# Grouped attention: queries for four batches at once, and values times probabilities in three rounded products

## The reference, cut to what matters

```python
def _L2_xattn_ref(text_hidden, vision_tokens, vision_mask, Wq, Wk, Wv, Wo):
    ...
    q = (text_hidden @ Wq).reshape(B, T_text, N_HEADS, HEAD_DIM).transpose(0, 2, 1, 3)
    k = (vision_tokens @ Wk).reshape(B, T_vis, N_KV_HEADS, HEAD_DIM).transpose(0, 2, 1, 3)
    v = (vision_tokens @ Wv).reshape(B, T_vis, N_KV_HEADS, HEAD_DIM).transpose(0, 2, 1, 3)
    ...
    scores = jnp.einsum('bhtd,bhsd->bhts', q, k) / scale
    mask = vision_mask[:, None, None, :]
    scores = jnp.where(mask, scores, -jnp.inf)
    attn = jax.nn.softmax(scores, axis=-1)
    ...
    out = jnp.einsum('bhts,bhsd->bhtd', attn, v)
    out = out.transpose(0, 2, 1, 3).reshape(B, T_text, N_HEADS * HEAD_DIM)
    return out @ Wo
```

## Time and profile before

| | us |
|---|---|
| median of 3 runs | 1918.61 |
| lowest, highest | 1918.14, 1919.21 |
| the profiled execution's own time | 1918.69 |
| its span | 1916.8 |
| first block of grouped attention | 1239.9 to 1258.2 |
| second block, first query matmul | 1258.24 |
| second block, first scores | 1269.92 |
| layer norm after it begins | 1449.9 |

### The profile page before, as it was taken

The page is one execution under the profiler, slowest core; times in us unless marked ns, Lnnn a source line. Parts: engine busy times, 40 slices in busy tenths (PEclk is TensorE's granted clock), DMA queues, the critical chain, the costliest instruction groups (busy, mean ns, idle before and its releaser), DMA issues. The chain is left out here.

```text
span 1916.8 us, 32156 instructions
## 1 busy us (share of the span) xinstructions
PE 1604.5 (84%) x11677; PEld 1182.8 (62%) x11677; DVE 1411.8 (74%) x2370; ACT 802.5 (42%) x1261; POOL 528.5 (28%) x594
## 2 busy tenths in 40 slices
PE   7899999999898986465858779899995998898864
PEld 5678888888784663122536445687773885645631
DVE  3299999999565855899487764556684995657697
ACT  3367666766232545333234312433342002425544
POOL 2234443433242511577112103200000330414200
PEclk9899999999898988688979989999997999998985
DMA  3000000000000000000100020000001220010000
GB/s 149 28 29 27 25 25 27 20 26 14 12 1 13 2 8 36 0 0 0 47 3 2 28 110 4 12 18 12 12 19 55 73 70 28 4 59 2 1 1 23
DMA packets 18145, 49.24 MB, mean 26 GB/s; under 512 B 2035, under 2 KB 8436, under 8 KB 16886
## 3 DMA queue, kind: packets, MB, share of 16 engines
q1 hardware_dynamic: 18038, 47.78, 7.3%
HBM read 46.73 MB, written 1.05 MB: 25 GB/s over the span
## 5 line engine op out<-in xcount | busy, mean ns | idle before, releaser
L2183 DVE SCALAR_TENSOR_TENSOR arena<-psum,arena 128x1016 f32<-128x1016 f32 (+2 forms) x240 | 303.4, 1265 | 35.9 <-ACT arena L2120 30.2
L902 DVE TENSOR_REDUCE limits<-psum 128x4 f32<-128x512 f32 (+2 forms) x256 | 147.9, 619 | 81.7 <-PE psum L757 49.2
L2029 PE MATMUL psum<-ssm_XT_hi,ssm_split 128*128 128x512 f32 x640 | 194.6, 407 | 11.7 <-POOL ssm_split L1988 5.7
L870 ACT ACTIVATE PT<-psum 128x1024 f32<-128x1024 f32 x112 | 108.6, 1021 | 115.0 <-PE psum L788 115.0
L2029 PEld LDWEIGHTS psum<-ssm_XT_hi,ssm_split 128*128 128x128 f32 x640 | 116.3, 192 | 37.0 <-POOL ssm_split L1988 10.9
L2120 ACT ACTIVATE arena<-psum,arena 128x1024 f32<-128x1024 f32 x80 | 89.1, 1114 | 106.0 <-PE psum L2029 104.7
L2606 PE MATMUL psum<-expert,x 128*128 128x256 f16 x1024 | 114.0, 276 | 16.7 <-POOL expert L2592 16.7
L757 PE MATMUL psum<-K,QR 32*128 32x256 f32 (+1 forms) x320 | 118.4, 443 | 7.8 <-DVE limits L902 6.4
L2783 POOL TENSOR_TENSOR fed<-dtx,b_all 128x1024 f32<-128x1024 f32 x32 | 103.2, 3243 | 65.1 <-DVE state L2852 33.4
L2606 PEld LDWEIGHTS psum<-expert,x 128*128 128x128 f16 x1024 | 101.1, 99 | 29.5 <-issue 16.8
L2619 DVE SCALAR_TENSOR_TENSOR acc<-psum,gate_now,acc 128x256 f32<-128x256 f32 x256 | 111.9, 483 | 7.7 <-PE psum L2606 7.6
(11 more groups left out here) (446 smaller groups left out, 3857.8 us busy)
## 6 DMA issues: line engine op xcount, KB each, us to landing
expert_mask<-in_expert_masks SPq DMA_DIRECT2D x32, 256.0 KB, 2.6
arena<-in_ssm_in SPq DMA_DIRECT2D x16, 384.0 KB, 3.0
arena<-in_L_xattn SPq DMA_DIRECT2D x1, 5120.0 KB, 15.8
arena<-in_ssm_in SPq DMA_DIRECT2D x16, 256.0 KB, 3.0
arena<-in_L_ffn SPq DMA_DIRECT2D x1, 2592.0 KB, 8.9
arena<-in_L_xattn SPq DMA_DIRECT2D x2, 1280.0 KB, 9.6
arena<-in_L_ffn SPq DMA_DIRECT2D x1, 2176.0 KB, 8.4
ssm_gated<-in_ssm_z SPq DMA_DIRECT2D x4, 512.0 KB, 5.8
```

Of the source, the lines that this page charges most:

```text
L870: nc.scalar.activation(PT[:, u % 2, 2 * k:2 * k + 2, :, :].rearrange("p r h q -> p (r h q)"), p.psum[:, (2 + 2 * k) * 512:(4 + 2 * k) * 51 ...
L902: ins = nc.vector.tensor_reduce(limits[:, u % 2, r, :, k], score_bank(r)[:, :].rearrange("p (h k) -> p h k", h=4)[:, :, lo:hi], AX.X, ALU. ...
L2029: ins = nc.tensor.matmul(bank[tile_bank(r, tile) + half][:, :], w_part(tile, kw, c), x_part(kx, c, slice(half * 512, (half + 1) * 512)), s ...
L2183: ins = nc.vector.scalar_tensor_tensor(out[:, :, ago:], product[:, :, :P - ago], tap, out[:, :, ago:], ALU.mult, ALU.add)
```

## The change

Queries are made per head for four batches at once: six matmuls of 512 columns a set in place of twelve of 256. A has one buffer, [16 heads, 4 x 128 queries]. All 16 heads of the first four batches are made ahead of the loop, with six banks in turn; the other four batches' are made in passes 12 to 15, four sets each, all in bank 6. Passes 0 to 11 and 16 to 31 have no queries.

Values times probabilities is three fp32r matmuls: hi x hi, hi x lo, lo x hi. The values are split at the end of the first block (ScalarE copy, then VectorE subtraction). The probabilities are split in the loop: ScalarE writes the rounded part from PSUM, ahead of its exponentials, and VectorE, where it had the copy, subtracts that part from PSUM, which now waits for ScalarE's copy. OT lies in the place of the fp32 values; the weight jobs' buffers lie in XT and in the place of the key weights.

```diff
-        A = sb("A_g", [P, 2, H, 2 * P])
+        A = sb("A_g", [P, H, 4 * P])
...
-        probsT = sb("probsT_g", [P, 2, 4 * P])
-        OT = sb("OT_g", [P, 2, 4, P])
-        stage = sb("w_stage", [P, 2, HID])
-        big = sb("w_big", [P, HID])
+        probsT_hi = sb("probsT_hi_g", [P, 2, 4 * P], F32R)
+        probsT_lo = sb("probsT_lo_g", [P, 2, 4 * P], F32R)
+        values_hi = sb("values_hi_g", [P, B, P], F32R)
+        values_lo = sb("values_lo_g", [P, B, P], F32R)
+        OT = values[:, :, :].rearrange("p (r h) t -> p r h t", r=2)
+        stage = p.XT[:, :, :].rearrange("p c t -> p (c t)")[:, :2 * HID].rearrange("p (r n) -> p r n", r=2)
+        big = p.w("wk")[:, :HID]
...
-        scores, psumT, psumO, psumA = bank[0:2], bank[2:4], bank[4:6], (lambda j, t: bank[6 if j else t][:, :])
+        scores, psumT, psumO, psumA = bank[0:2], bank[2:4], bank[4:6], (lambda j, h: bank[6 if j else (6, 7, 4, 5, 2, 3)[h % 6]][:, :])
...
+                act.wait_ge(s.operands_ready.sem, s.operands_ready.at(0))
+                nc.scalar.copy(values_hi[:, :, :], values[:, :, :]).then_inc(s.split_ready.up(), 1)
...
+                dve.wait_ge(s.split_ready.sem, s.split_ready.at(0))
+                nc.vector.tensor_tensor(values_lo[:, :, :], values[:, :, :], values_hi[:, :, :].bitcast(F32), ALU.subtract)
...
-                def queries(j, t):
-
-                    n = 8 * j + t
+                def queries(j, h):
+
+                    n = H * j + h
                     if j:
                         pe.wait_ge(s.tile_out_dve.sem, s.tile_out_dve.at(n - 1))
-                    cols = slice(2 * j * P, (2 * j + 2) * P)
-                    for h in (2 * t, 2 * t + 1):
-                        for km, kx, c in ALL:
-                            ins = nc.tensor.matmul(psumA(j, t)[:, h % 2 * 2 * P:(h % 2 + 1) * 2 * P], M[:, km, h, c, :], x_part(kx, c, cols),
-                                                   start=(km, kx, c) == ALL[0], stop=(km, kx, c) == ALL[-1])
+                    elif h >= 6:
+                        pe.wait_ge(s.tile_out_dve.sem, s.tile_out_dve.at(h - 6))
+                    cols = slice(4 * j * P, (4 * j + 4) * P)
+                    for km, kx, c in ALL:
+                        ins = nc.tensor.matmul(psumA(j, h), M[:, km, h, c, :], x_part(kx, c, cols),
+                                               start=(km, kx, c) == ALL[0], stop=(km, kx, c) == ALL[-1])
                     ins.then_inc(s.tile_ready.up(), 1)
...
-                    nc.tensor.matmul(psumO[n % 2][:, :], values[:, n // G, :], probsT[:, n % 2, :], start=True, stop=True
+                    nc.tensor.matmul(psumO[n % 2][:, :], values_hi[:, n // G, :], probsT_hi[:, n % 2, :], start=True, stop=False)
+                    nc.tensor.matmul(psumO[n % 2][:, :], values_hi[:, n // G, :], probsT_lo[:, n % 2, :], start=False, stop=False)
+                    nc.tensor.matmul(psumO[n % 2][:, :], values_lo[:, n // G, :], probsT_hi[:, n % 2, :], start=False, stop=True
                                      ).then_inc(s.pv_done.up(), 1)
...
-                for t in range(8):
-                    queries(0, t)
+                for h in range(H):
+                    queries(0, h)
                 for n in range(N + 4):
+                    second = 4 * (n - 12) if 12 <= n < N // 2 else None
                     if n < N:
                         score(n)
-                    if n + 8 < N:
-                        queries(n // 8 + 1, n % 8)
+                    if second is not None:
+                        queries(1, second)
                     if 2 <= n < N + 2:
                         turn(n - 2)
+                    if second is not None:
+                        queries(1, second + 1)
                     if 4 <= n:
                         onwards(n - 4)
+                    if second is not None:
+                        queries(1, second + 2)
                     if 3 <= n < N + 3:
                         read(n - 3)
+                    if second is not None:
+                        queries(1, second + 3)
...
                 for n in range(N + 3):
+                    if 2 <= n < N + 2:
+                        act.wait_ge(s.probsT_psum.sem, s.probsT_psum.at(n - 2))
+                        nc.scalar.copy(probsT_hi[:, n % 2, :], psumT[n % 2][:, :]).then_inc(s.high_ready.up(), 1)
                     if n < N:
                         act.wait_ge(s.negmax_ready.sem, s.negmax_ready.at(n))
-                        if n >= 2:
-
-                            act.wait_ge(s.probsT_psum.sem, s.probsT_psum.at(n - 2))
...
-                    if n + 8 < N:
-                        queries_out(n // 8 + 1, n % 8)
+                    if second is not None:
+                        queries_out(1, second)
                     if n >= 2:
-                        dve.wait_ge(s.probsT_psum.sem, s.probsT_psum.at(n - 2))
+                        dve.wait_ge(s.high_ready.sem, s.high_ready.at(n - 2))
                         if n >= 4:
 
                             dve.wait_ge(s.pv_done.sem, s.pv_done.at(n - 4))
-                        nc.vector.tensor_copy(probsT[:, n % 2, :], psumT[n % 2][:, :]).then_inc(s.probsT_ready.up(), 1)
+                        nc.vector.tensor_tensor(probsT_lo[:, n % 2, :], psumT[n % 2][:, :], probsT_hi[:, n % 2, :].bitcast(F32), ALU.subtract
+                                                ).then_inc(s.probsT_ready.up(), 1)
+                    if second is not None:
+                        queries_out(1, second + 1)
...
+                    if second is not None:
+                        queries_out(1, second + 2)
+                        queries_out(1, second + 3)
```

More of the change, by code:

```diff
@@ L289 @@
     "probs_ready", "probsT_psum", "probsT_ready", "pv_done", "operands_ready", "out_ready", "y_ready",
-    "moments_ready", "deviation_ready", "bias_added", "xq_ready", "hby_ready", "v_ready", "angle_ready", "const_loaded", "wo_loaded", "rest_loaded", "first_loaded", "relu_ready", "terms_ready", "term_product", "factor_ready", "shift_ready", "x_odd_ready", "x_ready", "xT_psum", "oT_psum", "oT_ready", "stored",
+    "moments_ready", "deviation_ready", "bias_added", "high_ready", "xq_ready", "hby_ready", "v_ready", "angle_ready", "const_loaded", "wo_loaded", "rest_loaded", "first_loaded", "relu_ready", "terms_ready", "term_product", "factor_ready", "shift_ready", "x_odd_ready", "x_ready", "xT_psum", "oT_psum", "oT_ready", "stored",
     "scaled_ready", "xqT_psum", "xqT_ready", "gu_ready", "gu_taken", "gate_scaled", "silu_ready", "hq_ready",
@@ L1217, in score @@
                     b, g = divmod(n, G)
-                    pe.wait_ge(s.tile_out_dve.sem, s.tile_out_dve.at(8 * (b // 2) + 2 * g + 1))
+                    pe.wait_ge(s.tile_out_dve.sem, s.tile_out_dve.at(H * (b // 4) + 4 * g + 3))
                     if n >= 2:
@@ L1223, in score @@
                     for h in range(4):
-                        ins = nc.tensor.matmul(scores[n % 2][:, h * P:(h + 1) * P], A[:, b // 2 % 2, 4 * g + h, b % 2 * P:(b % 2 + 1) * P],
+                        ins = nc.tensor.matmul(scores[n % 2][:, h * P:(h + 1) * P], A[:, 4 * g + h, b % 4 * P:(b % 4 + 1) * P],
                                                p.ctxT[:, b * P:(b + 1) * P], start=False, stop=(h == 3))
@@ L1302, in rounded, with queries_out @@
                     round_fp8(p, dve, fp8.of(n), stage[:K, n % 2, :cols], big[:K, :cols]).then_inc(s.wq_ready.up(), 1)
-                def queries_out(j, t):
-                    dve.wait_ge(s.tile_ready.sem, s.tile_ready.at(8 * j + t))
-                    nc.vector.tensor_copy(A[:, j % 2, 2 * t:2 * t + 2, :].rearrange("p h q -> p (h q)"), psumA(j, t)).then_inc(s.tile_out_dve.up(), 1)
+                def queries_out(j, h):
+                    dve.wait_ge(s.tile_ready.sem, s.tile_ready.at(H * j + h))
+                    nc.vector.tensor_copy(A[:, h, :], psumA(j, h)).then_inc(s.tile_out_dve.up(), 1)
                 def add(b):
@@ L1310, in add @@
                     nc.vector.tensor_tensor(p.X[:, b, :], p.X[:, b, :], psumY, ALU.add).then_inc(s.out_ready.up(), 1)
-                for t in range(8):
-                    queries_out(0, t)
+                for h in range(H):
+                    queries_out(0, h)
                 for n in range(N + 2):
+                    second = 4 * (n - 12) if 12 <= n < N // 2 else None
                     if n >= 8 and n % 4 == 0:
```

## The result

The changed kernel takes 1921.92 us (median of 20 runs, 1916.47 to 1923.89), the kernel before 1918.47 (median of 20, 1916.56 to 1919.53). The ratio is 1.0016, 95% interval 1.0009 to 1.0023: 3.1 us longer, between 1.7 and 4.4 (the medians themselves lie 3.45 apart). The middle of the interval is a small loss, under the 0.2% (3.8 us) that the prediction took as no change. Forecast were 1919.5 us and a range of 1913.5 to 1925.5.

What follows compares the result with a forecast made beforehand. The prediction took TensorE's issue order to bound the stage, so TensorE slots plus new gaps add up: 1.2 + 10.2 - 34.6 + 21.9 + 3.8 + 3.1 - 5.6 + 0.8 = +0.8 us, giving 1919.5 us, range 1913.5 to 1925.5.

Steps and rivals of the forecast that it cites:

- (a): End of the first block: the values' subtraction on VectorE lies beside nothing and adds 1.2 us (1.1 to 1.6).
- (b): First queries ahead of the loop: 96 matmuls of 512 columns at 0.228 us, nothing hides them, +10.2 us.
- (c), (d): Queries taken out of 24 passes at 1.44 us, -34.6 us; second queries in passes 12 to 15, +21.9 us.
- (e): Passes 12 to 15: second queries share bank 6 and wait for VectorE's evictions, +3.8 us (0 to 7).
- (f): Start of the loop: without queries TensorE waits for the first exponentials and scaling, +3.1 us (0 to 5).
- (g): Values times probabilities: three fp32r matmuls replace two fp32 passes, -0.175 us in each of 32 groups, -5.6 us.
- (h): VectorE's subtraction behind ScalarE's rounding copy: 0 in the body with 0.25 us margin, +0.8 us at the drain (0 to 2).
- (1): Rival for the loop: older work fills the new waits, 5.1 us faster than before, 1913.6 us; chance 0.17.
- (2): Rival for the fp32r matmuls: pace 0.216 us in place of 0.228, -3.5 us, 1916.0 us; chance 0.05.
- (3): Rival for the loop: VectorE, waiting for ScalarE's copy, becomes the bound, +6 us, 1925.5 us; chance 0.13.
- (4): Rival for the read: rounded products save nothing as three weight loads are exposed, 1925.1 us; chance 0.06.
- (5): Rival for the thinner start of the loop: the clock falls to 1.2 GHz, +5 us, 1924 us; chance 0.04.

Runs made afterwards that it cites:

- early split: Changed kernel with the values' rounding copy and subtraction put ahead of the first block's evictions of onward weights: stage 210.00 us, 1917.74 us in one run.
- spread: Changed kernel with the 16 second query sets laid over passes 12 to 18 (3, 3, 2, 2, 2, 2, 2): 1915.18 us, ratio to before 0.9986.
- Addition ahead: Changed kernel with VectorE's addition to X moved to the end of the pass before, ahead of the weight job: stage 210.17 us, 1917.29 us in one run.
- scaled first: Changed kernel with VectorE scaling group n-1 ahead of its subtraction for group n-2: stage 209.46 us, 1918.93 us in one run.
- late copy: Changed kernel with an extra, unused ScalarE copy of the transposed probabilities ahead of the rounding copy: stage 214.17 us, 1923.16 us in one run.
- reads only: Changed kernel with queries as before, so only the rounded three-matmul read is new: 1914.87 us, ratio to before 0.9973.
- queries only: Kernel before with only the new queries for four batches, the read left as one fp32 product: 1922.48 us, ratio to before 1.0018.

## Why the prediction was right

The forecast was +0.8 us, the stage gives +2.1, the ratio +3.1 and the medians +3.5. The cancelling of large terms and the outcome, no change by more than 0.2%, were right, and so was the mechanism, a sum of TensorE's slots and of new gaps. That the small remainder came out above zero is not to the credit of the working: its terms missed by up to 1.3 us each, more than the 0.8 forecast, and partly made up for one another. Step by step:

(a) End of the first block: +1.2 forecast, +1.28 measured (19.59 against 18.31), and early split took it all back. Right, with its reason.

(b) First queries: +10.2 forecast, +10.30 measured. The pace taken from another stage's rows (rows 7) held: 21.98 us for 96 matmuls, 0.229 each. The paces of 0.216 and with it the rival of a faster fp32r fall.

(c), (d) In the passes without queries the 1.44 us are gone as forecast. In the kernel spread two sets in a pass cost 7.06 - 4.27 = 2.79, 0.2325 a matmul with the seams; 0.228 was taken.

(e) Waits among the second queries: the step that failed in size. Forecast +3.8; four passes of 10.80 against 9.74 of work give 4.2, and pass 16 another 0.8, in sum +5.1. Of the 4.2 the waits for the bank were forecast well: with the seams of 0.2325 a matmul the work is 9.85 and the waits are 3.8. What the step missed is the work behind: VectorE does the last copy, then the job, then the addition to X, for which the next batch's products wait. I had counted the addition nowhere as a wait of TensorE. Addition ahead shows it (pass 16 back at 4.28).

(f) Start of the loop: +3.1 forecast, +2.4 measured (passes 0 to 4 sum to 13.9 us; before they sum to 19.0, less 7.2 of queries and 0.3 of the read that is 11.4). The waits are 1.0 and 0.8 where 1.26 and 1.25 were drawn, and the third is 0.3 where 0.57 was. The work of ScalarE and VectorE was drawn right: four exponentials took 1.5, the rounding copy 0.59, reciprocal and scaling 0.9. What was drawn short is TensorE's own part, 1.22 for a pass of scores alone where it takes 1.41, in both kernels; that time is no wait, and the change doesn't add it. How much of the 0.7 this explains stays open.

(g) The read: 0.163 us a group (4.430 less 4.267 for a pass) in place of 0.175, so -5.2 in place of -5.6.

(h) Nothing in the body: right, and scaled first shows it (9 us of VectorE's waiting for the copy removed, no pass of the body shorter). But a quarter microsecond of margin did not mean what the step said. With the copy half a microsecond later (late copy) the ordinary passes still stood at 4.27; the first thing to give was the addition every fourth pass. The +0.8 for the large jobs at the end was met in size, but only in part by the wait that was drawn. The first turn of the drain does wait 0.4 us for its scaling, and the drain, with four cheaper reads, ends 0.3 us nearer to the last scores instead of 0.6. The larger part, 0.53, is pass 28, which waits for the late addition; that it made up the sum is luck.

These sum to +1.28 + 10.30 - 34.6 + 22.0 + 5.1 + 2.4 - 5.2 + 0.9 = +2.2 against 2.1 measured. The stage misses the forecast by 1.3 us; term (e) alone is 1.3 too small, while (f), 0.7 too large, and (g), 0.4 too small a gain, nearly make up for each other. The rest of the difference, about 1 us, has no place in the traces.

The rivals: (1), the waits are filled, falls with four passes of 10.80. (2), the faster pace, falls with 0.229. (3), VectorE as the bound, falls with late copy. (4), a read that saves nothing, falls with reads only. (5), the clock at its lower level in the start of the loop, did not happen in the changed kernel's two profiles, which show 1.00 there. But it can: queries only shows 3.4 us of it at just that place, for 0.85 to 1.6 us. Both kernels had TensorE busy 2.88 of the 3.89 us ahead of it, so comparing busy shares, as the prediction did, could not settle this rival.

## What to carry to other kernels

Matmuls twice as long and half as many gain little here: two of 256 columns take 0.244 us and one of 512 takes 0.229, which is 2.2 us over the stage. And the filling work that had lain between dependent steps was lost with the old placement. When a batch of work is put in one place, draw the passes around it for every buffer that another engine must empty, the accumulator of the next step too, and space the sets by the time of one copy. And a wait of an engine that isn't the bound was free in the body of this loop and cost 1.9 us at its start and end: order its instructions there by who waits for them.

## What the runs showed that I had not expected

The stage repeats within 0.1 us from profile to profile (211.33, 211.23), while the same instructions outside it took between 1703.1 and 1707.6 us, as far apart as the effects looked for. The changed kernel's 20 runs spread over 7.4 us, those of before over 3.0, and among the changed kernel's the three fastest (1916.5 to 1917.2) have a mean granted clock of 0.920 to 0.923 and the runs above 1923 have 0.915; in its two profiles the stage has the full clock in all parts but the first block. Nor is the stage always at the full clock: of thirteen profiles one, queries only, had its clock at the lower level for 3.4 us of the loop, so a stage must be read together with its granted clock. With so small a change, the trace of the stage tells more than the medians.
